# Routed stages: the output pairs' weight spreads come by DMA, as the experts' do, with 16 buffers and reads sent twelve units ahead

## The reference, cut to what matters

```
x = x + 0.5 * ffn(layernorm(x))        # layer 0: 8 experts, top 2
x = x + attention(layernorm(x))        # layer 1
x = x + 0.5 * ffn(layernorm(x))        # layer 2
x = x + 0.5 * routed(layernorm(x))     # layer 3: 16 experts, the stage of the change
x = x + scan(layernorm(x))             # layer 4: selective scan
x = x + 0.5 * routed(layernorm(x))     # layer 5: the same stage again
```

```
rw = softmax(masked gating logits)                       # (token, 16)
q  = sum_e rw[t, e] * (h[t] @ q_proj[e])                  # 64 wide; k and v alike
attn = softmax(causal(q @ k.T) / 8) @ v
out = sum_e (rw[t, e] * attn[t]) @ o_proj[e]
```

## Time and profile before

| | us |
|---|---|
| median of three runs | 1728.18 (1726.42 to 1730.58) |
| the profiled execution | 1722.91 |
| its span | 1721.1 |
| PE busy | 1474.2 (86%) |
| DVE busy | 1208.4 (70%) |
| ACT busy | 585.2 (34%) |
| L1057, expert matmuls | 370.4 busy, 2048 matmuls |
| L1060, pair matmuls | 129.8 busy, 1024 matmuls |
| weight reads L449 | 256 of 256 KB, 4.2 and 4.9 from issue to landing (medians) |
| L1487, products with DMA or PSUM weights | 85.4 + 84.5 and 87.6 busy, 128 each |

### The profile page before, as it was taken

One profiled execution on the slowest core, in us unless ns is written; L12 is line 12 of the kernel. 1 busy time (PEld: TensorE's weight loads), 2 busy tenths in 40 slices (PEclk: granted clock), 3 DMA queues, 4 the chain that ended last, 5 costly groups with the idle time before them and its releaser, 6 DMA issues.

```text
span 1721.1 us, 22005 instructions
## 1 busy us (share of the span) xinstructions
PE 1474.2 (86%) x7582; PEld 1070.7 (62%) x7582; DVE 1208.4 (70%) x2729; ACT 585.2 (34%) x1131; POOL 435.7 (25%) x368
## 2 busy tenths in 40 slices
PE   3997885895999999976888878878887589999998
PEld 3894554795899999842343333333332289999996
DVE  3666663665676666424989898898989767676763
ACT  2203443200222222114646556565565212222221
POOL 1130000001000000004656576565666200000000
PEclk9998997897999999976999989998899889999998
DMA  4000000002232333200000000000000043333330
GB/s 131 1 1 1 1 1 1 1 1 99 99 100 99 101 117 110 70 1 1 0 1 1 1 1 1 0 1 0 1 1 1 6 169 112 121 106 105 105 106 13
DMA packets 49581, 76.76 MB, mean 45 GB/s; under 512 B 6775, under 2 KB 15934, under 8 KB 49342
## 3 DMA queue, kind: packets, MB, share of 16 engines
q1 hardware_dynamic: 49470, 75.35, 13.4%
HBM read 72.71 MB, written 2.62 MB: 44 GB/s over the span
## 4 chain that ended last, share of the span: by engine, by line
PE 63%; DVE 15%; issue 13%; ACT 4%; POOL 3%; DMA 1%; DVEq 0%; POOLq 0%; ACTq 0%
PE bank L1057 20%; PE bank L1060 7%; PE bank L914 5%; PE bank L1183 5%; DVE hs L1550 3%; PE bank L950 2%; PE bank L1017 2%; DVE xe L1550 2%; PE bank L1119 2%; DVE both L1542 2%; PE bank L1002 2%; PE bank L1069 2%; POOL both L539 2%; PE bank L999 1%; PE bank L959 1%
## 5 line engine op out<-in xcount | busy, mean ns | idle before, releaser
L1057 PE MATMUL bank<-wqkv_sb,xe 128*128 128x192 f32 x2048 | 370.4, 334 | 10.5 <-DVE xe L1487 10.3
L1057 PEld LDWEIGHTS bank<-wqkv_sb,xe 128*128 128x128 f32 x2048 | 340.1, 194 | 21.9 <-DVE xe L1487 15.4
L1183 PE MATMUL bank<-both,ident 128*128 128x512 f32 x512 | 265.2, 619 | 3.0 <-DVE both L1542 3.0
L507 POOL TENSOR_TENSOR rstd<-ve,half_neg 128x4 f32<-128x4 f32 x32 | 37.5, 1173 | 769.8 <-DVE ve L1238 769.8
L794 ACT ACTIVATE bank<-dt,A 128x512 f32<-128x512 f32 x256 | 174.5, 687 | 145.2 <-DVE xe L1550 95.0
L539 POOL TENSOR_TENSOR both<-du,prob 128x512 f32<-128x512 f32 x128 | 161.6, 1269 | 102.2 <-DVE xe L1550 56.6
L539 POOL TENSOR_TENSOR both<-du,prT 128x512 f32<-128x512 f32 x128 | 161.5, 1271 | 58.8 <-DVE hs L1550 33.8
L1550 DVE TENSOR_TENSOR_SCAN xe<-bank,both 128x512 f32<-128x512 f32 x128 | 155.3, 1213 | 5.5 <-ACT bank L794 5.2
L1550 DVE TENSOR_TENSOR_SCAN hs<-bank,both 128x512 f32<-128x512 f32 x128 | 155.1, 1212 | 2.1 <-ACT bank L794 2.1
L1183 PEld LDWEIGHTS bank<-both,ident 128*128 128x128 f32 x512 | 97.9, 198 | 86.7 <-issue 54.6
L914 PEld LDWEIGHTS bank<-exp_sb,xe 128*128 128x128 f32 x1024 | 138.3, 197 | 5.0
(11 more groups left out here) (271 smaller groups left out, 2134.5 us busy)
## 6 DMA issues: line engine op xcount, KB each, us to landing
dt<-w_rows SPq DMA_DIRECT2D x128, 256.0 KB, 4.2
du<-w_rows SPq DMA_DIRECT2D x128, 256.0 KB, 4.9
xs<-in_x_dram SPq DMA_DIRECT2D x8, 256.0 KB, 3.7
out_dram<-xs SPq DMA_DIRECT2D x8, 256.0 KB, 2.5
wqkv_sb<-in_wqkv_dram SPq DMA_DIRECT2D x1, 1536.0 KB
exp_sb<-in_expT_dram SPq DMA_DIRECT2D x1, 512.0 KB, 4.9
wo_sb<-in_wo_dram SPq DMA_DIRECT2D x1, 512.0 KB
win_sb<-in_W_in_dram SPq DMA_DIRECT2D x1, 256.0 KB
```

Of the source, the lines that this page charges most:

```text
L507: pool.tensor_tensor(rstd[:], ve[:], half_neg[:, 0:NT], ALU.pow).then_inc(ln_rstd, 1)
L1057: m = pe.matmul(bank[4 + j // 2][:, (j % 2) * 3 * HD:(j % 2 + 1) * 3 * HD], x_e, wqkv_sb[:, e, :], start=(e == 0 and j % 2 == 0), stop=(e ...
L1183: pe.matmul(bank[4 + k % NH][:], ident[:], hc[k % HRING], start=False, stop=(SUM_RANK[k] == sums_of(k // UNITS, k % NH))).then_inc(hc_used, 1)
```

## The change

All 24 units of a batch now get their weights by DMA. A pair unit's tile comes in two reads of 128 KB, one row to 64 partitions each. There are 16 buffers (`dt`, `du`, `g2`, `u2` of the scan), taken in turn by all units, and a read is sent when its unit's slot is at most twelve ahead; it waits for the product 16 units before it. The spreads of PE, the three-part split of DVE, the second turn and the second copy of ACT are gone. The semaphores `rows_ps` and `rows_made` are gone too; `wT_ps` and `wT_sb` stand in for them. The steps' slots move: PE turns `wts` after slot 17 (it was 16), ACT copies the rows in slot 18 (it was 17), and SP's write of the rows stands straight ahead of the first read of that batch.

```diff
-SLOTS = 8
-LOOK = 5
+SLOTS = 16
+LOOK = 12
...
-        wide = [t[:, h, :] for t in dt_ + du for h in range(NH)]
+        wide = [t[:, h, :] for t in dt_ + du + g2 + u2 for h in range(NH)]
...
             def rows_to_dram(r, b):
-                sp.wait_ge(rows_made, seen(r * NB + b + 1))
+                sp.wait_ge(wT_sb, seen(2 * NB + r * NB + b + 1))
...
                 if n >= SLOTS:
-                    sp.wait_ge(xe_made, seen(expert_before(r, m)))
-                sp.dma_start(wide[n % SLOTS], w_rows[r * NB + c, e:e + 1, :].to_broadcast([P, L])).then_inc(wide_in[n % SLOTS], 16)
+                    sp.wait_ge(xe_made, seen(2 * FFN + n + 1 - SLOTS))
+                if e < E2:
+                    sp.dma_start(wide[n % SLOTS], w_rows[r * NB + c, e:e + 1, :].to_broadcast([P, L])).then_inc(wide_in[n % SLOTS], 16)
+                else:
+                    for k in range(2):
+                        row = NH * (e - E2) + k
+                        sp.dma_start(wide[n % SLOTS][k * HD:(k + 1) * HD, :], w_rows[r * NB + c, row:row + 1, :].to_broadcast([HD, L])).then_inc(wide_in[n % SLOTS], 16)
...
-                    if (u - 18) % UNIT == 0 and 0 <= (u - 18) // UNIT + 1 < NB:
-                        rows_to_dram(r, (u - 18) // UNIT + 1)
-                    while sent < NB * E2 and sent // E2 * UNIT + sent % E2 <= u + LOOK:
+                    while sent < NB * UNIT and clock_of(sent) <= u + LOOK:
+                        if clock_of(sent) % UNIT == 0 and clock_of(sent) < UNIT * NB:
+                            rows_to_dram(r, clock_of(sent) // UNIT)
                         widen(r, sent)
                         sent += 1
...
-                    act.activation(rows_sb[b % 2], bank[1][0:E2, :], ACT.Copy).then_inc(rows_made, 1)
-                    yield
-                    act.wait_ge(wT_ps, seen(2 * NB + n + 1))
-                    act.wait_ge(bc_ps, seen(2 * FFN + PAIRS * max(0, n - 2)))
-                    act.activation(wT3[b % 3][:], bank[1][0:W3, 0:L // 2].bitcast(BF16), ACT.Copy).then_inc(wT_sb, 1)
+                    act.activation(rows_sb[b % 2], bank[1][0:E2, :], ACT.Copy).then_inc(wT_sb, 1)
                     yield
...
-                steps = by_clock(front, (6, 14, 17, 19), back, (18, 22, 23, 25, 26, 28, 29, 31, 32, 34))
+                steps = by_clock(front, (6, 14, 18), back, (18, 22, 23, 25, 26, 28, 29, 31, 32, 34))
...
-                    m.then_inc(rows_ps, 1)
-                    yield
-                    pe.wait_ge(w3_made, seen(2 * n + 2))
-                    pe.wait_ge(rows_made, seen(n + 1))
-                    parts = bank[1][0:W3, 0:L // 2].bitcast(BF16)
-                    for j in range(NT):
-                        m = pe.transpose(parts[:, j * P:(j + 1) * P], w3[:, j, :], identb[:])
                     m.then_inc(wT_ps, 1)
...
-                    pe.matmul(bank[2 + p % 2][:], pick2[:, k, :, :].rearrange("p a c -> p (a c)"), wT3[c % 3][:], start=True, stop=True).then_inc(bc_ps, 1)
-
-                steps = by_clock(front, (5, 7, 16, 18), back, (18, 20, 23, 26, 28, 29, 30, 31, 32, 33))
+                steps = by_clock(front, (5, 7, 17), back, (18, 20, 23, 26, 28, 29, 30, 31, 32, 33))
...
-                    three_parts(wts[:], rem[:], w3, E2, w3_made)
...
-                steps = by_clock(front, (0, 1, 3, 4, 10, 11, 12, 13, 15, 16), back, (22, 25, 28, 31, 37, 50))
+                steps = by_clock(front, (0, 1, 3, 4, 10, 11, 12, 13, 15), back, (22, 25, 28, 31, 37, 50))
...
-                            w = bank[2 + (e - E2) % 2][:]
-                        dve.tensor_tensor(xe[i % RING][:], xnT[b % 2][:] if e < E2 else at2[:], w, ALU.mult).then_inc(xe_made, 1)
+                        dve.tensor_tensor(xe[i % RING][:], xnT[b % 2][:] if e < E2 else at2[:], wide[slot], ALU.mult).then_inc(xe_made, 1)
```

More of the change, by code:

```diff
@@ L82, with wide_count @@
 CLOCK = range(-UNIT, UNIT * (NB + 1) + 8)
-SLOTS = 8
-LOOK = 5
-def expert_before(r, m):
-    r, m = divmod(r * NB * E2 + m - SLOTS, NB * E2)
-    return experts_at(r, m // E2) + m % E2 + 1
+SLOTS = 16
+LOOK = 12
+def wide_count(r, i):
+    n = r * NB * UNIT + i
+    return sum(1 if clock_of(m % (NB * UNIT)) % UNIT < E2 else 2 for m in range(n % SLOTS, n + 1, SLOTS))
 def due(gens, u):
@@ L346, in macaron @@
         rows_out = plain("rows_out")
-        rows_ps, rows_made = sem("rows_ps"), sem("rows_made")
         wide_in = [plain(f"wide_in{i}") for i in range(SLOTS)]
@@ L437, in rows_to_dram, with widen @@
             def rows_to_dram(r, b):
-                sp.wait_ge(rows_made, seen(r * NB + b + 1))
+                sp.wait_ge(wT_sb, seen(2 * NB + r * NB + b + 1))
                 sp.dma_start(w_rows[r * NB + b], rows_sb[b % 2]).then_inc(rows_out, 16)
-            def widen(r, m):
-                n = r * NB * E2 + m
-                c, e = divmod(m, E2)
+            def widen(r, i):
+                n = r * NB * UNIT + i
+                b, e = divmod(clock_of(i), UNIT)
+                c = b if e < E2 else b - 1
                 if e == 0:
@@ L684, in front @@
                     yield
-                    act.wait_ge(rows_ps, seen(n + 1))
+                    act.wait_ge(wT_ps, seen(2 * NB + n + 1))
                     if n > 1:
                         act.wait_ge(rows_out, 16 * (n - 1))
-                    act.activation(rows_sb[b % 2], bank[1][0:E2, :], ACT.Copy).then_inc(rows_made, 1)
-                    yield
-                    act.wait_ge(wT_ps, seen(2 * NB + n + 1))
-                    act.wait_ge(bc_ps, seen(2 * FFN + PAIRS * max(0, n - 2)))
-                    act.activation(wT3[b % 3][:], bank[1][0:W3, 0:L // 2].bitcast(BF16), ACT.Copy).then_inc(wT_sb, 1)
+                    act.activation(rows_sb[b % 2], bank[1][0:E2, :], ACT.Copy).then_inc(wT_sb, 1)
                     yield
@@ L977, in front @@
                     yield
-                    pe.wait_ge(w3_made, seen(2 * n + 1))
+                    pe.wait_ge(w3_made, seen(n + 1))
                     for j in range(NT):
                         m = pe.transpose(bank[1][0:E2, j * P:(j + 1) * P], wts[:, j, :], ident[:])
-                    m.then_inc(rows_ps, 1)
-                    yield
-                    pe.wait_ge(w3_made, seen(2 * n + 2))
-                    pe.wait_ge(rows_made, seen(n + 1))
-                    parts = bank[1][0:W3, 0:L // 2].bitcast(BF16)
-                    for j in range(NT):
-                        m = pe.transpose(parts[:, j * P:(j + 1) * P], w3[:, j, :], identb[:])
                     m.then_inc(wT_ps, 1)
@@ L1062, in unit @@
                     m.then_inc(xe_used, 1)
[L1064 to L1068, removed]
-                    pe.matmul(bank[2 + p % 2][:], pick2[:, k, :, :].rearrange("p a c -> p (a c)"), wT3[c % 3][:], start=True, stop=True).then_inc(bc_ps, 1)
-                steps = by_clock(front, (5, 7, 16, 18), back, (18, 20, 23, 26, 28, 29, 30, 31, 32, 33))
+                steps = by_clock(front, (5, 7, 17), back, (18, 20, 23, 26, 28, 29, 30, 31, 32, 33))
                 for u in CLOCK:
                     i = unit_at(u)
-                    ahead = unit_at(u + AHEAD)
-                    if ahead is not None and (u + AHEAD) % UNIT >= E2:
-                        spread((u + AHEAD) // UNIT - 1, (u + AHEAD) % UNIT - E2)
                     if i is not None:
@@ L1442, in front @@
                     dve.wait_ge(wT_ps, seen(2 * NB + n))
-                    dve.wait_ge(rows_ps, seen(n))
                     link(dve.tensor_tensor(wts[:], ex[:], eq[:], ALU.mult))
@@ L1447, in front @@
                     dve.tensor_tensor(wts[:], wts[:], over(den[:], E2), ALU.mult).then_inc(w3_made, 1)
-                    yield
-                    dve.wait_ge(w3_made, seen(2 * n + 1))
-                    three_parts(wts[:], rem[:], w3, E2, w3_made)
                     yield
@@ L1478, in routed @@
                             dve.wait_ge(at_sb, seen(r * NB + b))
+                        slot = (r * NB * UNIT + i) % SLOTS
+                        dve.wait_ge(wide_in[slot], 16 * wide_count(r, i))
                         dve.wait_ge(xe_used, seen(base + i + 1 - RING))
[L1480 to L1485, removed]
-                            w = bank[2 + (e - E2) % 2][:]
-                        dve.tensor_tensor(xe[i % RING][:], xnT[b % 2][:] if e < E2 else at2[:], w, ALU.mult).then_inc(xe_made, 1)
+                        dve.tensor_tensor(xe[i % RING][:], xnT[b % 2][:] if e < E2 else at2[:], wide[slot], ALU.mult).then_inc(xe_made, 1)
                     due(steps, u)
```

## The result

The changed kernel takes 1741.16 us, the median of 20 runs, where the kernel before, run beside it, has one of 1726.46 (1723.09 to 1733.38). One of the 20 runs took 2219.34 us at a mean granted clock of 0.62; it is left out of the ratio and of the range of the others, 1728.2 to 1746.5. The ratio, of the means, is 1.0066, with a 95% interval of 1.0047 to 1.0085: slower by 11 us (8 to 15), where +9.3 was forecast. The medians lie further apart, 14.7 us, since the 19 runs fall into two groups, seven of 1728.2 to 1734.2 and twelve of 1739.0 to 1746.5. The profiled execution is of the lower group: 1734.17 us with a span of 1732.3, 11.2 more than before's span.

The account below looks back on a forecast made before the run. PE, busy 40.00 of 40.00 us in a steady batch, was taken as the bound. Terms: -29.8 + 28.2 + 5.4 + 5.5 = +9.3 us on 1728.2, about 1737 us; the forecast's own range was 1731 to 1744.

Parts of the forecast that it names:

- What goes from PE: Routed layers: spreads and the turn L987 leave full PE, 14.9 us per layer, 29.8 us saved for two.
- The part in the last pairs: Last eight pairs of a layer: six spreads count as removed from PE, saving 1.3 us per layer.
- The chain: Changes into batches 2 to 7: next rows come late, PE waits, 2.35 us each, 28.2 us for two layers.
- The follow-on waits: Behind unit 24 at each change into batches 2 to 7: PE waits 0.20 and 0.71 us more.
- The clock: Changes into batches 2 to 7: PE's clock falls to half at six of twelve, 0.9 us each, 5.5 us.
- Rival 1: Changes of batch: the stalls come but the clock stays, 1732 us; chance 0.20.
- Rival 2: Changes of batch: the clock falls at each, 20 us in place of 5.5, 1752 us; chance 0.10.
- Into batch 1: Change into batch 1, no pairs to hide behind: rows' copy later, 2.7 us lost, 5.4 us for two layers.
- Rival 4: Changes of batch: rows are in time, all 28.2 us of waits go, faster at 1703 us; chance 0.12.

Follow-up runs that it names:

- Experiment 1: The changed kernel with ACT's copy of the rows one slot earlier (17), ahead of qT and kT: 1696.51 us, ratio 0.9842 against the kernel before.
- 2: The kernel before, with the turn of the weights and the rows' copy as late as in the change: 1758.86 us, ratio 1.0178.
- 7: The changed kernel with DVE's statistics two slots later, away from between the products of units 24 and 25: 1741.06 us, ratio 1.0085.
- 9: The changed kernel with five idle matmuls ahead of unit 24 and DVE's statistics two slots later: 1723.35 us, ratio 0.9970.
- experiment 4: The changed kernel with five idle float32 matmuls filling PE's gap ahead of unit 24: 1735.82 us, ratio 1.0041.
- 10: The changed kernel once more, unaltered, against the kernel before: 1737.81 us, ratio 1.0065.
- 5: The changed kernel with PE's turn after slot 16 and ACT's rows' copy in slot 17, as before the change: 1703.12 us, ratio 0.9868.
- experiment 3: The changed kernel with eight buffers and reads five slots ahead, late copy kept: 1741.16 us, ratio 1.0077.

## Why the prediction was right

It forecast 1737 us and slower; 1741.16 was measured, a difference of +11 for +9.3. The chain behind it is shown; that the two numbers lie so close is in part luck, as told below.

- **What goes from PE** (-29.8). Experiment 1 shows it without the stalls: 1.91 a batch for 1.98, -12.5 and -12.9 in the two layers for -14.9 (from the first expert matmul to the end of the last pair). The part in the last pairs did not come: in layer 3 they took 8.79 us, against 8.40 before, because PE now stands 1.83 us ahead of them, not 1.39, and the clock was 0.51 over 3.5 us of them. In experiment 1 they took 8.8 as well. The term was some 4 us too large.

```profile
747.50 8.79 PE L1054 MATMUL bank<-wo_sb,xe 128*128 128x128 f32 x64 [1.83 <-DVE xe L1462]
```

- **The chain.** Forecast and measured behind slot 16: write 5.59 and 5.60, product 10.47 and 10.36, PE's start 11.21 and 11.11, PE ready 9.77 and 9.91. So the gap was 1.20 for 1.44; ten of twelve are 1.20 to 1.49. The follow-on waits are 5.09 - 4.17 = 0.92 for 0.91. The prediction counted them at all twelve changes, but into batch 7 there is no coming batch whose statistics could stand between the products, and there they are absent, as the row below shows. Experiments 1 and 2 show the cause from both sides.

```profile
696.12 4.17 PE L1051 MATMUL bank<-wqkv_sb,xe 128*128 128x192 f32 x24 [1.28 <-DVE xe L1462]
```

- **The clock.** Falls at 7 of 12 for 6, at 0.7 to 1.1 us each for 0.9, except one of 7 us. What the prediction counted separately, the waits and the falls, are not independent, as it said for 0.91 us of them; experiments 7 and 9 show this. Rival 1 is refuted by gaps of 1.2 to 1.5 us with half clock behind them, at five of the ten changes with such a gap, and by experiment 4, where the same places without the gap have none. The reading of the Trainium skill ("TensorE: Matmul & The Clock Gate", "Why this matters for your kernels") by which gaps this short bring no fall does not agree with these rows. Rival 2 is refuted by the five changes without a fall; its 1752 was also too high, since it charged each fall 1.7 us on top of the waits that the fall swallows. That six falls of twelve were taken and seven came was an even guess that held: the same kernel fell at seven again in 10, with eight buffers at four.
- **Into batch 1** (+5.4). In layer 5 the layer's start moved by 0.83 us (1378.80 to 1379.63) and PE's first instruction behind batch 1's third unit by 3.50 (1417.81 to 1421.31): 2.67 us more, for 2.7. In layer 3 it is 2.9. There the clock is at half for 10.2 us in place of 6.8.

**What the prediction did not have: late writes.** At two of the twelve changes the gap was 2.08 and 2.37 us. The write of the rows landed in 2.5 us in place of 1.6, and the read, which waits for it, slipped with it:

```profile
1451.32 0.33 SPq L438 DMA_DIRECT2D w_rows<-th  x1
...
1453.81 0.33 SPq L450 DMA_DIRECT2D g<-w_rows  x1
```

```profile
DMA to landing us min/median/max: 2.5/2.5/2.5
```

```profile
1457.72 7.15 PE L1051 MATMUL bank<-wqkv_sb,xe 128*128 128x192 f32 x24 [2.08 <-DVE xe L1462]
```

With the 7-us fall behind the first of them these two batches take 43.40 and 42.35 us from write to write, some 3 us more than the 41.3 to 41.5 with a short fall. That is about half of why layer 5 lost 10.4 us where 4.65 was forecast, while layer 3 lost 4.5; another 2.3 are its last pairs, which took 9.37 us for 8.40 where 1.3 were to go. Layer 4, which the change does not touch, was 4.1 us shorter in this profile, one of its two lengths. So the nearness of the sum to +9.3 is in part luck: the routed layers of the profile lost 14.8 us, and layer 4 hid 4.1 of them. The terms that can be checked one by one are within 0.3 us at each change of batch with a usual write, except the 0.9 us into batch 7; the last pairs (some 4 us in both layers) and the late writes with the long fall (some 3) were not foreseen.

**Rival 4** (1703 us if the rows are in time) was about the right price for a case that did not come: experiment 1 has 1696.51, and 5 has 1703.12. What decides between it and the forecast is the order of ACT's steps, as the prediction said, not any speed.

## What to carry to other kernels

Freed time on a full engine is worth what the next chain of latencies leaves: lay the chain (turn, copy, write, read, product) out from one fixed start on the timelines, and do so against the new, shorter time of the engine that was full. When steps of two chains fall in one slot of a hand-written order, the one whose result goes through DRAM belongs first; here one slot number was worth 39 us (1.0066 against 0.9842). Removing a wait can gain nothing while the clock is at half over the same stretch, as in 7, so try the edit also with the clock held up, as in 9, before dropping it.

## What was unexpected of the hardware

- A write of 32 KB to DRAM lands in 1.6 us as a rule, but the read behind it followed 2.2 to 3.6 us after the write at 21 of 176 writes over the eleven profiles other than that of before, and at none of its 16. With slack ahead of the read this is invisible; in the changed kernel each one is a longer gap.
- The first of a burst of 256 KB reads lands in 3.0 to 3.8 us with eight or with 16 queued (once 4.6, in 9), where the groups of later ones have medians of 6.1 to 6.6 in the change: the length of the queue behind it makes no difference here.
- Gaps of PE of 1.2 to 1.5 us, with a full PE on both sides, were followed by half clock at five of ten places in the change, and those of 2.1 and 2.4 us at both. In experiment 3 it was four of the ten short ones and neither of two of 2.2 and 2.4 us. The same gap with five idle matmuls in it was followed by none in twelve.
